# Summing the states of a selective scan by f32 transposes in PSUM, and turning silu(z) instead of the gated result

## The chip, the cores and the metric

The program runs on one core of one Trainium2 chip. The metric is device time in microseconds (us); the kernel before took 230.39 us, the median of three runs (228.88 to 230.66).

## The reference

Two blocks stand one behind the other, for 4 sequences (batches) of 256 positions and 256 channels:

```python
x = x + mixer(ctx_1024, layernorm(x))     # z is layernorm(x)
x = x + ffn(layernorm(x))
# mixer, per batch: 256 channels, 16 states
u  = silu(causal_conv(in_proj(ctx)))
dt = softplus(dt_proj(x_proj(u)) + b)
state = state * exp(dt * A) + (dt * u) * B_t   # a scan over positions, 16 states
y  = sum over states of state * C_t
y  = (y + D * u) * silu(z)
# ffn: h = gelu(silu(quantised linear 256 -> 1024)); layer_norm; quantised linear 1024 -> 256
```

The change concerns the sum over states, the gate by silu(z), and the order of everything around them.

## The kernel before

Channels lie on partitions, in 2 halves (h) of 128; positions lie along the free dimension. The scan is cut into 32 units k: 4 batches (b), 2 halves, 4 groups of 4 states. A unit is 128 x 1024 (4 states x 256 positions), and goes through all engines:

- TensorE (PE): `scale_b(k)`, L474, writes dt*u*B into PSUM, two slots, so it waits for scan k-2;
- ScalarE (ACT): `exps(k)`, L613, four instructions, writes exp(dt*A) into a ring of 6 (`dA`), so it waits for scan k-6;
- VectorE (DVE): `scan(k)`, L909, writes `st`, a ring of 4, so it waits for the sum of unit k-4;
- GpSimd (POOL): `prod(k)`, L753, multiplies `st` by C;
- PE: `sum_states(k)`, L490, adds the four states into one PSUM bank by matmuls with an identity as the stationary operand; ahead of the first unit of each half one matmul with diag(D), L487, adds D*u.

When the four units of a half are summed, DVE multiplies the sum by silu(z) (`gate`, L926, once per half of a batch, out to `yg`), PE transposes the result to positions by channels (`turn_y`, L504, two transposes per call), and DVE adds it to x (`add_x1`, L931). After both halves `ln1` takes statistics, `quant1` quantises, and the FFN runs on tiles t of 128 positions, 8 in all, two per batch: PE `turn_q1`, `mm1` (L527 for the bias, L531); ACT `silu` (L646) and `gelu` (L650), each with a function table of its own; DVE `bn2` (L984); POOL `root2a`; ACT `norm` (L656); DVE `gain` (L1002); POOL `shift` (L789); ACT `square` (L665) and DVE `amax2` (L1009); POOL `root2b`; DVE `scales2`; ACT `scale2` (L671); POOL `quant2`; PE `turn_q2`, ACT `copy_q2` (L678), PE `mm2`, DVE `res`, and a store. ACT computes silu(z) per batch in `silu_z` (L689). Every change of function on ACT to or from exp, silu or gelu loads a table (L707 is the load ahead of `exps`).

The order is written out by hand: for each engine a table (`VECTOR_AT`, `SCALAR_AT`, `POOL_AT`, `PE_AT`) with a row for each unit. An engine does its own part of unit k-1, then what row k names:

```python
for k in range(UNITS + 1):
    if k:
        scan(k - 1)
    for name, i in steps(VECTOR_AT, k):
        work[name](i)
```

Engines run their rows in that order and wait on semaphores only. The last row (32) holds all that stands behind the last scan. One PSUM bank, `head`, is shared by the small PE products and is handed on by `take`; the pair of banks `big` serves `mm1`, `turn_q2` and the convolution.

Of the kernel before, what the change touches and what calls it, by code (L numbers as in the profile page):

```python
# [15 lines left out]
BF16 = mybir.dt.bfloat16  # L16
# [41 lines left out]
    "dt_neg:2 x1:0",
    "spread_b:4 spread_b:5",
    "spread_b:6",  # L60
    "spread_b:7 gate:1 dt_mask:2 dt_sum:2",
# [3 lines left out]
    "x1:1 ln1:0 wmean:0",  # L65
    "spread_b:8 spread_b:9 spread_b:10",
    "gate:2",
    "spread_b:11 clip_weights:0 clip_weights:1 quant1:0 dt_neg:3",
    "gate:3",
    "x1:2 dt_mask:3",  # L70
    "x1:3 ln1:1 bn2:0 dt_sum:3",
# [2 lines left out]
    "quant1:1",
    "gain:0 bn2:1 gate:4",
    "x1:4 spread_b:12 spread_b:13 amax2:0 spread_b:14 bn2:2 gain:1",
    "scales2:0 amax2:1",
    "spread_b:15 gate:5",
    "x1:5 bn2:3 scales2:1 ln1:2",
    "quant1:2 gain:2",  # L80
    "amax2:2 gain:3",
    "bn2:4 scales2:2 amax2:3 gate:6",
    "scales2:3",
    "bn2:5 gain:4 x1:6 gate:7 x1:7 ln1:3 res:0 quant1:3 res:1 amax2:4 scales2:4 gain:5 amax2:5 res:2 "
    "bn2:6 scales2:5 gain:6 res:3 amax2:6 bn2:7 scales2:6 gain:7 quant2:6 res:4 amax2:7 scales2:7 res:5 "
    "quant2:7 res:6 res:7",
)
SCALAR_AT = (
    "silu_u:1",
    "",  # L90
    "copy_xd:1 sum_weights:0",
    "dt_bias:1",
    "copy_half:1",
    "dt_exp:1 silu_u:2",
    "silu_z:0 copy_xd:2 silu_z:1",
    "copy_du:1 dt_bias:2 silu_z:2 dt_exp:2",
# [11 lines left out]
    "silu_u:3",
    "scale_weights:1 copy_xd:3 silu_z:3",
    "dt_bias:3 copy_q1:0 dt_exp:3",  # L110
    "silu:0 gelu:0",
    "norm:0 silu:1 gelu:1 copy_du:3",
    "copy_q1:1",
    "",
    "silu:2 square:0 norm:1 gelu:2 silu:3",
    "",
    "scale2:0 square:1 gelu:3",
    "scale2:1 copy_q2:0 norm:2",
    "norm:3 copy_q2:1",
    "copy_q1:2 square:2 silu:4 gelu:4 square:3 scale2:2",  # L120
    "silu:5 scale2:3 gelu:5 norm:4 square:4 copy_q2:2 norm:5 copy_q2:3 copy_q1:3 scale2:4 silu:6 gelu:6 "
    "square:5 silu:7 scale2:5 gelu:7 square:6 copy_q2:4 scale2:6 copy_q2:5 square:7 copy_q2:6 scale2:7 "
    "copy_q2:7",
)
POOL_AT = (
    "",
    "",
    "",
    "dt_series:1",
    "",  # L130
    "",
    "dt_series:2",
# [981 lines left out]
```

## Time and profile before

| | |
|---|---|
| median of 3 runs | 230.39 us |
| the profiled execution's own time | 231.39 us |
| its span | 229.6 us |
| busy: PE, DVE, ACT, POOL | 193.3, 189.1, 175.3, 144.9 us |
| first scan starts, last scan (unit 31) starts | 26.13, 179.9 us |
| last gate starts | 189.45 us |

The span can be read in three parts: up to 22.7 us inputs arrive and batch 0 is prepared; from there to 179.9 us the 31 scans ahead of the last one and the work between them; and 49.7 us from the last scan's start to the end, where what is left of the FFN runs. Busy time is what an engine spent in its instructions; it is a share of the span and says nothing by itself about which engine ended a wait.

### The profile page before, as it was taken

To read this page: it belongs to the slowest core of one execution; us is meant where nothing else is said; L and a number is where in the kernel's file an instruction comes from. 1 tells how busy PE (TensorE), PEld (TensorE's weight loads), DVE (VectorE), ACT (ScalarE), POOL (GpSimd) and SP (SyncE) were. 2 spreads that over 40 slices of the span, in tenths; PEclk is the share of its full clock that TensorE was granted. 3 is DMA by queue.
4 is the path that set the end of the run, shared out by engine and by line. 5 is a ranking of instruction groups with operands and counts; after the bars stand their busy time and mean duration, and the time that the engine had idled before them with its cause. 6 is when DMAs were issued, how large, how long until landed. Compare 5 with 4: busy or idle time off the path is not lost.

```text
span 229.6 us, 2849 instructions
## 1 busy us (share of the span) xinstructions
PE 193.3 (84%) x886; PEld 146.0 (64%) x886; DVE 189.1 (82%) x266; ACT 175.3 (76%) x269; POOL 144.9 (63%) x142
## 2 busy tenths in 40 slices
PE   3298989989999999999999999939999965892472
PEld 2076668768777898786867877828865753341351
DVE  0985897989999999986999979799999658746861
ACT  2164969988970898897959989996988955779751
POOL 0040037834772976601969099999599998968871
PEclk9999999999999999999999999997999999599569
DMA  6639930004040005410000204300000000100011
GB/s 186 227 85 383 421 144 6 0 0 166 26 178 0 0 0 174 139 58 0 3 0 3 93 6 150 121 0 0 0 0 0 3 0 0 47 23 1 24 46 49
DMA packets 7135, 15.85 MB, mean 69 GB/s; under 512 B 904, under 2 KB 4432, under 8 KB 6992
## 3 DMA queue, kind: packets, MB, share of 16 engines
q1 hardware_dynamic: 6528, 14.90, 18.4%
q10 hardware_dynamic: 592, 0.77, 1.2%
q8 instruction: 7, 0.11, 0.2%
q14 instruction: 8, 0.07, 0.1%
HBM read 14.56 MB, written 1.11 MB: 68 GB/s over the span
## 4 chain that ended last, share of the span: by engine, by line
PE 27%; DVE 21%; POOL 19%; ACT 19%; issue 10%; DMA 1%; POOLq 0%; DVEq 0%; ACTq 0%
POOL st L753 9%; DVE st L909 8%; PE ps L490 6%; ACT dA L613 6%; PE ps L474 6%; PE ps L405 4%; ACT L707 3%; PE ps L527 2%; POOL sm L780 2%; POOL w_raw L789 2%; ACT L689 2%; ACT siluz L689 2%; DVE diagB L894 2%; PE ps L424 1%; DVE sp_mask L856 1%
## 5 line engine op out<-in xcount | busy, mean ns | idle before, releaser
L753 POOL TENSOR_TENSOR st<-st,bc 128x1024 f32<-128x1024 f32 x32 | 75.7, 2374 | 42.7 <-DVE st L909 42.4
L909 DVE TENSOR_TENSOR_SCAN st<-dA,ps 128x1024 f32<-128x1024 f32 x32 | 72.4, 2275 | 3.0 <-PE ps L474 1.6
L474 PE MATMUL ps<-diagB,dtuT 128*128 128x256 f32 x256 | 62.5, 390 | 1.5 <-DVE dtuT L902 0.6
L490 PE MATMUL ps<-st,id_f 128*128 128x256 f32 x256 | 59.7, 381 | 2.3 <-POOL st L753 2.3
L474 PEld LDWEIGHTS ps<-diagB,dtuT 128*128 128x128 f32 x256 | 48.0, 194 | 11.7 <-issue 3.3
L490 PEld LDWEIGHTS ps<-st,id_f 128*128 128x128 f32 x256 | 48.0, 190 | 10.1 <-POOL st L753 3.9
L613 ACT ACTIVATE dA<-dt,negA 128x255 f32<-128x255 f32 x128 | 53.0, 495 | 0.1
L894 DVE TENSOR_TENSOR diagB<-id_f,ps 128x1024 f32<-128x1024 f32 x16 | 18.8, 1202 | 1.5 <-PE ps L424 1.5
L789 POOL TENSOR_TENSOR w_raw<-w_raw,rows_sb 128x1024 f32<-128x1024 f32 x6 | 14.1, 2354 | 7.2 <-DVE w_raw L1002 7.2
L527 PE MATMUL ps<-rows_sb,diag 128*128 128x512 f32 x32 | 17.2, 662 | 0.4 <-ACT w_raw L646 0.4
L984 DVE BATCH_NORM_STATS2 stats<-w_raw 128x6 f32<-128x512 f32 x16 | 10.3, 683 | 6.0 <-ACT w_raw L650 6.0
L538 PE MATMUL ps<-id_b,q 128*128 128x128 bf16 x64 | 6.2, 253 | 10.5 <-ACT q2T L678 6.7
L1009 DVE TENSOR_REDUCE am<-w_raw 128x1 f32<-128x1024 f32 x8 | 9.7, 1216 | 5.9 <-POOL w_raw L789 4.7
L665 ACT ACTIVATE junk<-w_raw 128x1024 bf16<-128x1024 f32 x8 | 8.4, 1050 | 7.6 <-POOL w_raw L789 6.7
L405 PE MATMUL ps<-ctx_sb,taps_sb 128*128 128x256 f32 (+3 forms) x48 | 13.5, 443 | 0.0
L707 ACT ACT_TABLE_LOAD x10 | 12.8, 1283 | 0.2
L538 PEld LDWEIGHTS ps<-id_b,q 128*128 128x128 bf16 x64 | 4.8, 113 | 12.3 <-ACT q2T L678 7.2
L545 PE MATMUL ps<-w2q,q2T 128*128 128x256 bf16 x64 | 10.3, 314 | 2.5 <-DVE res L1034 1.9
L405 PEld LDWEIGHTS ps<-ctx_sb,taps_sb 128*128 128x128 f32 x48 | 10.8, 229 | 2.5 <-issue 0.7
L671 ACT ACTIVATE w_raw<-w_raw,sm 128x1024 f32<-128x1024 f32 x8 | 9.1, 1144 | 3.5 <-DVE sm L1020 3.5
L646 ACT ACT_TABLE_LOAD x8 | 10.3, 1283 | 0.1
L650 ACT ACT_TABLE_LOAD x8 | 10.3, 1283 | 0.1
(120 smaller groups left out, 295.2 us busy)
## 6 DMA issues: line engine op xcount, KB each, us to landing
bc<-spread SPq DMA_DIRECT2D x16, 512.0 KB, 3.6
rows_sb<-rows SPq DMA_DIRECT2D x1, 1664.0 KB, 14.3
x_nat<-x SPq DMA_DIRECT2D x2, 512.0 KB, 7.3
w_raw<-w1T SPq DMA_DIRECT2D x1, 1024.0 KB, 9.0
w_raw<-w2T SPq DMA_DIRECT2D x1, 1024.0 KB, 11.0
out<-res SPq DMA_DIRECT2D x8, 128.0 KB, 1.7
taps_sb<-taps ACTq DMA_DIRECT2D x1, 512.0 KB, 4.9
ctx_sb<-ctxT SPq DMA_DIRECT2D x1, 384.0 KB, 5.5
```

The costliest lines, as they stand in the source:

```text
L405: mm = nc.tensor.matmul(xin(b)[:, h * L + s:(h + 1) * L], inw_taps[:, s, h * P:(h + 1) * P], ctx_sb[:, b * L:(b + 1) * L - s], start=s == ...
L474: mm = nc.tensor.matmul(o[:, i:i + 2, t, :], dtuT[:, b % 2, h, t, :], diagB[:, b % 2, t, n:n + 2, :], start=True, stop=True)
L490: mm = nc.tensor.matmul(yacc, id_f[:, :], st[:, k % ST_RING, i * L:(i + 1) * L], start=False, stop=ng == GROUPS - 1 and i == SG - 1)
L527: nc.tensor.matmul(big[:, c], diag[:, i, :], rows_sb[:, c], start=True, stop=False)
L538: mm = nc.tensor.transpose(tq2[:, k * P:(k + 1) * P], q2[:, t % 2, k * P:(k + 1) * P], id_b[:, :])
L545: mm = nc.tensor.matmul(mm2, q2T[:, t % 2, k, :], w2q[:, k, :], start=k == 0, stop=k == KB - 1)
L613: e = nc.scalar.activation(dA[:, k % DA_RING, i * L + 1:(i + 1) * L], dt[:, h, b % 2, 1:L], ACT.Exp, scale=negA[:, h, n:n + 1])
L707: nc.scalar.preload_act_table_set("natural_log_exp_and_others")
L753: tt(s, s, bc[:, ng].rearrange("p s l -> p (s l)"), ALU.mult).then_inc(prod_done, 1)
L789: tt(h, h, rows_sb[:, 2 * HID:3 * HID], ALU.add).then_inc(shifted, 1)
L894: tt(diagB[:, b % 2, :, n, :], id_f[:, :].unsqueeze(1).unsqueeze(1).to_broadcast([P, TPB, SG, P]), b_cols_of(b)[:, :, n].unsqueeze(3).to_b ...
L909: nc.vector.tensor_tensor_scan(st[:, k % ST_RING, :], dA[:, k % DA_RING, :], slot(k), 0.0, ALU.mult, ALU.add).then_inc(scanned, 1)
```

## The change

The sum over states is made with positions on partitions. Each 128 x 128 block of `st` becomes the stationary operand of an f32 transpose with the identity moving, and eight such transposes per unit accumulate into one bank `yT`, [positions, 2 tiles, 256 channels], which serves both halves. D*u goes there by two matmuls per half. The bank is freed once per batch instead of once per half.

silu(z) is turned instead: PE `turn_z` makes four transposes per batch, ACT `copy_z` copies them to `siluzT`; `gate` and `add_x1` are now per position tile, and `add_x1` reads only SBUF. `turn_y` is gone. `siluz` holds one batch, so `silu_z(b)` waits for `turn_z(b-1)` and is called four times at different places. The scratch output of `square` lies in `taps_sb`, and the last two tiles' shift and quantisation count on semaphores of their own. All four order tables are written anew; of them one line each stands here.

```diff
 VECTOR_AT = (
-    "spread_b:1 spread_b:2",
-    "spread_b:3 dt_half:1",
+    "spread_b:1 dt_half:1",
+    "spread_b:2",
...
 SCALAR_AT = (
-    "silu_u:1",
+    "silu_z:0 silu_u:1",
...
-        yacc = bank(0)[:, 0:L]
+        yT = bank(0).rearrange("p (t d) -> p t d", t=TPB)
...
-                    else:
-                        pe.wait_ge(gate_step, k // GROUPS)
+                    elif h == 0:
+                        pe.wait_ge(gate_step, TPB * b)
                     pe.wait_ge(u_ready, b + 1)
-                    nc.tensor.matmul(yacc, diag_D[:, h, :], u[:, h, b, :], start=True, stop=False)
+                    for t in range(TPB):
+                        nc.tensor.matmul(yT[:, t, h * P:(h + 1) * P], u[:, h, b, t * P:(t + 1) * P], diag_D[:, h, :],
+                                         start=h == 0 and t == 0, stop=False)
                 pe.wait_ge(prod_done, k + 1)
                 for i in range(SG):
-                    mm = nc.tensor.matmul(yacc, id_f[:, :], st[:, k % ST_RING, i * L:(i + 1) * L], start=False,
-                                          stop=ng == GROUPS - 1 and i == SG - 1)
+                    for t in range(TPB):
+                        o = i * L + t * P
+                        mm = nc.tensor.matmul(yT[:, t, h * P:(h + 1) * P], st[:, k % ST_RING, o:o + P], id_f[:, :],
+                                              is_transpose=True, start=False,
+                                              stop=h == 1 and ng == GROUPS - 1 and i == SG - 1 and t == TPB - 1)
                 mm.then_inc(summed, 1)
...
-            def turn_y(g):
-                take("head", x1_half, g + 1)
-                pe.wait_ge(gate_step, g + 1)
-                for i in range(TPB):
-                    mm = nc.tensor.transpose(yT[:, i * P:(i + 1) * P], yg[:, g % 2, i * P:(i + 1) * P], id_f[:, :])
-                mm.then_inc(y_turned, 1)
+            def turn_z(b):
+                take("head", zT_done, b + 1)
+                pe.wait_ge(z_ready, HALVES * (b + 1))
+                for t in range(TPB):
+                    for h in range(HALVES):
+                        mm = nc.tensor.transpose(head[:, t * D + h * P:t * D + (h + 1) * P],
+                                                 siluz[:, h, t * P:(t + 1) * P], id_f[:, :])
+                mm.then_inc(z_turned, 1)
...
+            def copy_z(b):
+                act.wait_ge(z_turned, b + 1)
+                nc.scalar.activation(siluzT[:, b].rearrange("p t d -> p (t d)"), head, ACT.Copy).then_inc(zT_done, 1)
+
             def silu_z(b):
                 act.wait_ge(z_small, 4)
+                if b:
+                    act.wait_ge(z_turned, b)
...
-                tt(yg[:, g % 2, :], yacc, siluz[:, h, b, :], ALU.mult).then_inc(gate_step, 1)
+            def gate(i):
+                b, t = i // TPB, i % TPB
+                dve.wait_ge(summed, UPB * (b + 1))
+                dve.wait_ge(zT_done, b + 1)
+                if i >= TPB:
+                    dve.wait_ge(x1_half, i - TPB + 1)
+                tt(yg[:, t, :], yT[:, t, :], siluzT[:, b, t, :], ALU.mult).then_inc(gate_step, 1)
+
+            def add_x1(i):
+                b, t = i // TPB, i % TPB
+                dve.wait_ge(gate_step, i + 1)
+                tt(x_nat[:, t, b, :], x_nat[:, t, b, :], yg[:, t, :], ALU.add).then_inc(x1_half, 1)
```

What the new tables do to the order is seen on ACT around the last `exps`. Before (L613 is `exps`, L707 its table load, L665 `square`, L646 `silu`, L650 `gelu`, L671 `scale2`, L656 `norm`), the last `exps` is the second L613 row:

```order
L678 ACTIVATE q2T<-ps 128x1024
L613 ACTIVATE dA<-dt,negA 128x255 x4
L636 ACTIVATE q1T<-ps 128x512
L665 ACTIVATE junk,sm<-w_raw 128x1024
L646 ACT_TABLE_LOAD
L646 ACTIVATE w_raw<-ps,sm 128x1024
L650 ACT_TABLE_LOAD
L650 ACTIVATE w_raw<-w_raw 128x1024
L665 ACTIVATE junk,sm<-w_raw 128x1024
L671 ACTIVATE w_raw<-w_raw,sm 128x1024
L707 ACT_TABLE_LOAD
L613 ACTIVATE dA<-dt,negA 128x255 x4
```

Now, in the changed kernel, the same place (L630 is `exps`, L732 its load, L663 `silu`, L667 `gelu`, L690 `scale2`, L673 `norm`, L684 `square`):

```order
L653 ACTIVATE q1T<-ps 128x512
L663 ACT_TABLE_LOAD
L663 ACTIVATE w_raw<-ps,sm 128x1024
L667 ACT_TABLE_LOAD
L667 ACTIVATE w_raw<-w_raw 128x1024
L690 ACTIVATE w_raw<-w_raw,sm 128x1024
L673 ACTIVATE w_raw<-w_raw,sm 128x1024
L732 ACT_TABLE_LOAD
L630 ACTIVATE dA<-dt,negA 128x255 x4
L684 ACTIVATE taps_sb,sm<-w_raw 128x1024
L663 ACT_TABLE_LOAD
L663 ACTIVATE w_raw<-ps,sm 128x1024
```

Three tiles' silu and gelu (2, 3 and 4) now stand in one block ahead of the last `exps` with none of the other `exps` between them, and `square` of tile 2 has moved behind it. Over the whole program ACT has 27 table loads where it had 35.

On PE, before, the last units (L474 `scale_b`, L527 and L531 `mm1`, L504 `turn_y`, L487 the D matmul, L490 `sum_states`):

```order
L527 MATMUL ps<-rows_sb,diag 128x512 x2
L531 MATMUL ps<-w1q,q1T 128x512 x4
L474 MATMUL ps<-diagB,dtuT 128x2x128 x4
L490 MATMUL ps<-st,id_f 128x256 x4
L527 MATMUL ps<-rows_sb,diag 128x512 x2
L531 MATMUL ps<-w1q,q1T 128x512 x4
L474 MATMUL ps<-diagB,dtuT 128x2x128 x4
L504 MATMUL ps<-id_f,yg 128x128 x2
L474 MATMUL ps<-diagB,dtuT 128x2x128 x4
L487 MATMUL ps<-cv,diag_D 128x256
L490 MATMUL ps<-st,id_f 128x256 x16
```

Now, on PE in the changed kernel (L484 `scale_b`, L532 `turn_q1`, L544 and L548 `mm1`, L504 now the accumulating transposes, L498 the D matmuls):

```order
L484 MATMUL ps<-diagB,dtuT 128x2x128 x4
L532 MATMUL ps<-id_b,q 128x128 x4
L544 MATMUL ps<-rows_sb,diag 128x512 x2
L548 MATMUL ps<-w1q,q1T 128x512 x4
L484 MATMUL ps<-diagB,dtuT 128x2x128 x4
L504 MATMUL ps<-id_f,st 128x128 x8
L484 MATMUL ps<-diagB,dtuT 128x2x128 x8
L504 MATMUL ps<-id_f,st 128x128 x8
L544 MATMUL ps<-rows_sb,diag 128x512 x2
L548 MATMUL ps<-w1q,q1T 128x512 x4
L498 MATMUL ps<-diag_D,cv 128x128 x2
L504 MATMUL ps<-id_f,st 128x128 x32
```

`scale_b` of units 29, 30 and 31 stands directly behind tile 4's `turn_q1` and `mm1`, and the first FFN output transposes (`turn_q2`), of which two stood among the last units, all come behind the last sum.

At the start, on DVE, before (L894 `spread_b`, L856 to L876 one half of batch 0's softplus, `dt_half:1`, L909 `scan`):

```order
L902 COPY dtuT<-ps 128x256
L894 TENSOR_TENSOR diagB<-id_f,ps 128x2x512 x2
L909 SCALAR_TENSOR_TENSOR st<-dA,ps 128x1024
L894 TENSOR_TENSOR diagB<-id_f,ps 128x2x512
L856 TENSOR_SCALAR sp_mask<-sp_e 128x256
L858 TENSOR_SCALAR sp_ser<-sp_e 128x256
L860 TENSOR_TENSOR sp_ser<-sp_ser,sp_e 128x256
```

Now, in the changed kernel (L919 `spread_b`, L881 to L901 the half's softplus, L934 `scan`):

```order
L927 COPY dtuT<-ps 128x256
L919 TENSOR_TENSOR diagB<-id_f,ps 128x2x512
L881 TENSOR_SCALAR sp_mask<-sp_e 128x256
L883 TENSOR_SCALAR sp_ser<-sp_e 128x256
L885 TENSOR_TENSOR sp_ser<-sp_ser,sp_e 128x256
L892 COPY_PREDICATED sp_ln<-sp_mask,sp_ser 128x256
L898 SCALAR_TENSOR_TENSOR dt<-sp_v,sp_ln 128x256
L901 TENSOR_TENSOR dtu<-dt,cv 128x256
L934 SCALAR_TENSOR_TENSOR st<-dA,ps 128x1024
```

The second half's softplus has moved ahead of the first scan, and two `spread_b` behind it.

## Rows read from the trace of the kernel before

**Rows 1.** The page's part 1: busy time of each engine over the span.
```profile
PE 193.3 (84%) x886; PEld 146.0 (64%) x886; DVE 189.1 (82%) x266; ACT 175.3 (76%) x269; POOL 144.9 (63%) x142
```

**Rows 2.** The page's part 4: the chain that ended last, by engine.
```profile
PE 27%; DVE 21%; POOL 19%; ACT 19%; issue 10%; DMA 1%; POOLq 0%; DVEq 0%; ACTq 0%
```

**Rows 3.** Windows: length, busy PE, PEld, DVE, ACT, POOL, PEclk, DMA share, GB/s.
```profile
22.70:60.40 37.70, 34.89 (x161) 27.56 (x162) 33.53 (x27) 34.25 (x64) 19.14 (x11) 1.00 0.30 118
60.40:105.70 45.30, 44.52 (x209) 37.20 (x208) 42.18 (x50) 34.65 (x67) 25.03 (x14) 1.00 0.21 71
105.70:140.00 34.30, 33.83 (x154) 24.23 (x153) 32.85 (x45) 29.75 (x42) 24.23 (x22) 1.00 0.10 32
140.00:179.90 39.90, 35.70 (x166) 28.46 (x165) 37.01 (x53) 35.99 (x52) 35.71 (x36) 0.96 0.07 27
179.90:229.60 49.70, 30.14 (x166) 18.88 (x164) 30.83 (x58) 32.70 (x34) 37.48 (x50) 0.83 0.06 22
...
148.40:154.00 5.60, 1.91 (x10) 1.38 (x9) 5.05 (x5) 5.55 (x7) 5.34 (x4) 1.00 0.00 0
154.00:160.00 6.00, 6.00 (x27) 5.22 (x28) 5.90 (x14) 3.98 (x7) 5.42 (x9) 0.72 0.00 0
```

**Rows 4.** Timeline, PE: sums, transposes, mm1 at either clock (start, length, what).
```profile
75.08 0.60 PE L455 MATMUL ps<-id_f,dtu 128*128 128x128 f32 x4
79.45 1.89 PE L490 MATMUL ps<-st,id_f 128*128 128x256 f32 x8
116.72 1.88 PE L527 MATMUL ps<-rows_sb,diag 128*128 128x512 f32 x4
118.43 1.03 PE L531 MATMUL ps<-w1q,q1T 128*128 128x512 bf16 x4
197.12 3.73 PE L527 MATMUL ps<-rows_sb,diag 128*128 128x512 f32 x4
```

**Rows 5.** Timeline, DVE: two waits between 22.7 and 105.7 us.
```profile
39.80 2.29 DVE L909 TENSOR_TENSOR_SCAN st<-dA,ps 128x1024 f32<-128x1024 f32 x1 [1.59 <-PE ps L474]
105.06 0.69 DVE L851 SCALAR_TENSOR_TENSOR sp_e<-sp_v 128x512 f32<-128x512 f32 x1 [2.12 <-ACT sp_v L593]
```

**Rows 6.** Groups of instructions by line, ACT: busy and mean ns, idle before.
```profile
L707 ACT ACT_TABLE_LOAD x10 | 12.8, 1283 | 0.2
L625 ACT ACTIVATE dtuT<-ps 128x512 f32<-128x512 f32 x3 | 1.7, 581 | 8.0 <-PE ps L455 8.0
L646 ACT ACTIVATE w_raw<-ps,sm 128x1024 f32<-128x1024 f32 x8 | 8.9, 1114 | 1.7 <-PE ps L531 1.7
L650 ACT ACTIVATE w_raw<-w_raw 128x1024 f32<-128x1024 f32 x8 | 8.5, 1057 | 0.1
L656 ACT ACTIVATE w_raw<-w_raw,sm 128x1024 f32<-128x1024 f32 x6 | 7.4, 1232 | 3.3 <-POOL sm L782 3.3
L665 ACT ACTIVATE junk<-w_raw 128x1024 bf16<-128x1024 f32 x8 | 8.4, 1050 | 7.6 <-POOL w_raw L789 6.7 <-DVE w_raw L998 0.9
L671 ACT ACTIVATE w_raw<-w_raw,sm 128x1024 f32<-128x1024 f32 x8 | 9.1, 1144 | 3.5 <-DVE sm L1020 3.5
L678 ACT ACTIVATE q2T<-ps 128x1024 bf16<-128x1024 bf16 x8 | 8.1, 1010 | 2.8 <-PE ps L538 2.1 <-PE ps L545 0.7
```

**Rows 7.** Groups of instructions by line, DVE.
```profile
L909 DVE TENSOR_TENSOR_SCAN st<-dA,ps 128x1024 f32<-128x1024 f32 x32 | 72.4, 2275 | 3.0 <-PE ps L474 1.6 <-ACT dA L613 1.4
L931 DVE TENSOR_TENSOR x_nat<-x_nat,ps 128x256 f32<-128x256 f32 x8 | 3.2, 401 | 0.6 <-PE ps L504 0.6
L984 DVE BATCH_NORM_STATS2 stats<-w_raw 128x6 f32<-128x512 f32 x16 | 10.3, 683 | 6.0 <-ACT w_raw L650 6.0
L1002 DVE TENSOR_TENSOR w_raw<-w_raw,rows_sb 128x1024 f32<-128x1024 f32 x6 | 8.8, 1465 | 0.0
L1009 DVE TENSOR_REDUCE am<-w_raw 128x1 f32<-128x1024 f32 x8 | 9.7, 1216 | 5.9 <-POOL w_raw L789 4.7 <-POOL sm L812 1.2
```

**Rows 8.** Waits of ACT in the window 179.9 to 229.6 us.
```profile
ACT junk L665 <- POOL w_raw L789: 5.1, 1, 5.1
```

More of the change, by code:

```diff
@@ L51 @@
 VECTOR_AT = (
-    "spread_b:1 spread_b:2",
-    "spread_b:3 dt_half:1",
-    "dt_neg:1",
-    "",
-    "dt_mask:1 dt_sum:1",
-    "gate:0",
[L58 to L61, printed above, removed]
[35 rows of a table added]
+)
+SCALAR_AT = (
[6 rows of a table added]
     "",
@@ L64 @@
     "",
[L65 to L71, printed above, removed]
-    "",
-    "",
[L74 to L86, printed above, removed]
-)
-SCALAR_AT = (
-    "silu_u:1",
-    "",
[L91 to L96, printed above, removed]
[26 rows of a table added]
+)
+POOL_AT = (
+    "",
+    "",
+    "dt_series:1",
     "",
@@ L101 @@
     "",
-    "copy_du:2 sum_weights:1",
     "",
@@ L105 @@
     "",
-    "scale_weights:0",
     "",
[L108 to L132, printed above, removed]
+    "dt_series:2 root1:0 add_b2:0",
+    "dt_series:3",
     "",
@@ L137 @@
     "",
-    "add_b2:0 root1:0",
+    "root2a:0 add_b2:1 root1:1",
+    "",
+    "root2a:1 shift:0",
+    "",
+    "root2b:0",
+    "",
+    "",
+    "shift:1",
+    "root2b:1 root1:2 quant2:0 out_scale:0 root2a:2",
+    "",
+    "root2a:3 shift:2 quant2:1",
+    "",
+    "",
+    "root2b:2 shift:3 root2a:4 out_scale:1 root1:3 root2a:5 root2b:3 quant2:2 out_scale:2 shift:4 "
+    "quant2:3 add_b2:2 out_scale:3 root2a:6 root2b:4 shift:5 root2a:7 out_scale:4 root2b:5 root2b:6 "
+    "quant2:4 out_scale:5 quant2:5 root2b:7 out_scale:6 add_b2:3 out_scale:7",
+)
+PE_AT = (
+    "xdbl:1 dtraw:1 scale_b:1 turn_half:1 scale_b:2",
+    "turn_z:0 scale_b:3 scale_b:4 convolve:2 wsum:0 scale_b:5",
+    "",
+    "scale_b:6 turn_du:1",
+    "b_cols:1 scale_b:7",
+    "",
+    "scale_b:8",
+    "scale_b:9 turn_z:1",
+    "xdbl:2 scale_b:10 dtraw:2 scale_b:11 b_cols:2 convolve:3 scale_b:12 scale_b:13 xdbl:3",
+    "turn_du:2",
+    "dtraw:3",
+    "",
+    "turn_z:2 scale_b:14 scale_b:15 turn_q1:0",
+    "mm1:0 b_cols:3 scale_b:16 scale_b:17",
+    "",
+    "scale_b:18",
+    "scale_b:19 scale_b:20 mm1:1",
+    "",
+    "",
+    "scale_b:21",
+    "turn_du:3 scale_b:22",
+    "scale_b:23 turn_z:3 scale_b:24 scale_b:25 turn_q1:1",
+    "",
+    "",
+    "scale_b:26 mm1:2 scale_b:27",
+    "mm1:3",
+    "scale_b:28 turn_q1:2 mm1:4 scale_b:29",
+    "scale_b:30 scale_b:31",
+    "mm1:5",
     "",
@@ L548, in _ @@
             work = {"convolve": convolve, "wsum": wsum, "xdbl": xdbl, "dtraw": dtraw, "b_cols": b_cols, "turn_du": turn_du,
-                    "turn_half": turn_half, "turn_y": turn_y, "turn_q1": turn_q1, "mm1": do_mm1, "scale_b": scale_b,
+                    "turn_half": turn_half, "turn_z": turn_z, "turn_q1": turn_q1, "mm1": do_mm1, "scale_b": scale_b,
                     "turn_q2": turn_q2, "mm2": do_mm2}
```

103 lines of the change are left out of this document (24 added, 79 removed), and 60 rows, old and new, of tables (SCALAR_AT, VECTOR_AT).

## The prediction, made before the changed kernel was run

> **What bounds the kernel now.** I read the busy shares first [rows 1]: PE 84%, DVE 82%, ACT 76%, POOL 63%. No engine stands out, and the chain that ended last changes engine all the time [rows 2]. So the question goes to the stages, and the table by stretch answers it [rows 3]. I cut at the first row of the order tables (22.7 us) and at the start of the last scan (179.9 us). Between them lie 157.2 us, in which PE was busy 34.89+44.52+33.83+35.70 = 148.9, DVE 33.53+42.18+32.85+37.01 = 145.6, ACT 134.6 and POOL 104.1. PE and DVE are thus both nearly full: PE hardly waits between 60 and 140 us (78.4 of 79.6 busy), and DVE's idle time is only 157.2 - 145.6 = 11.6 us. The last stretch, 49.7 us, is another case: the busiest engine there (POOL) works 37.5 us, ACT 32.7, DVE 30.8. It is a chain of small steps between engines, and the sum over states has no part in it after its first 10 us.
>
> The reader should take one thing from this: the span is 22.7 + (DVE's work ahead of the last scan) + (DVE's idle time there) + (the rest after the last scan starts) = 22.7 + 145.6 + 11.6 + 49.7 = 229.6. Whatever PE or ACT save can shorten the span only through the 11.6 and the 49.7. The execution took 231.39 us on its own clock, 1.8 over its span, and 1.0 over the median of the runs.
>
> **The change part by part: PE.** A unit's sum took 1.89 us for 8 records of 256 columns [rows 4]. The new sum is 8 f32 transposes of 128 columns. The nearest row is L455, f32 transposes from SBUF: 4 in 0.60 us [rows 4]. One record lasts about 0.27 from start to end, so each further one adds (0.60-0.27)/3 = 0.11, and eight take 0.27 + 7 x 0.11 = 1.04 us. No row shows a transpose that accumulates. Bounds: 1.04 if accumulation is free, 1.89 (saving nothing) if it costs a second pass; below, nothing speaks for less. I take 1.04, since the row has the same operands and kind. Saved: 0.85 a unit; about 29 sums lie ahead of the last scan, 24.7 us. The D matmuls (one of 256 columns becomes two of 128) and `turn_z` against `turn_y` (4 x 4 transposes for 8 x 2) I take as even, within 1 us either way. PE's work ahead of the last scan falls from 148.9 to about 124. It stops being a bound, DVE does not.
>
> **ACT.** Eight table loads fewer (35 to 27), 8 x 1.283 = 10.3 us [rows 6]; four `copy_z` more at L625's 0.58, 2.3 us; the scattered `silu_z` and their loads are in that count. Net -8.0 us of 175.3.
>
> **DVE.** `gate` and `add_x1` stay 8 instructions each of 128 x 256, about 0.40 us [rows 7]. `add_x1` now has both operands in SBUF; I take no price. Bounds: nothing, or up to 0.5 us each where POOL works beside it, 4 us in all (L1002, two SBUF operands, ranges that way: its mean of 1.47 for 1024 elements is above L1009's 1.22). What counts is what the new order moves behind the last scan: `bn2:4` (2 x 0.68), `gain:3` (1.47), `amax2:3` (1.22), `gate:6` (0.40) and two pairs of tiny scale steps, together 4.8 us [rows 7]. DVE's work ahead of the last scan: 145.6 - 4.8 = 140.8.
>
> **DVE's idle time ahead of the last scan.** 22.7 to 60.4: 4.2 us, of which 1.59 is scan 3 waiting for its `scale_b`, which stood behind the 16 records of a convolution [rows 3, 5]. Now `scale_b:3` stands ahead of the convolution, and `dt_half:1` fills the gap ahead of scan 0: 1.5 left. 60.4 to 105.7: 3.1, of which 2.12 is `dt_neg:3` waiting for a bias step on ACT [rows 5]; it now stands after scan 12 with shorter queues on PE: 1.0 left. 105.7 to 140: 1.5, kept. 140 to 179.9: 2.9, and here a new wait arises. The block of silu and gelu for tiles 2 to 4 stands ahead of the last `exps`. From the end of `quant1:2` ACT needs a copy 0.58, `mm1:4` on PE 2.74 (116.72 to the end at 119.46 [rows 4]), silu 1.11, a load and gelu 2.34, scale2 1.14, norm 1.23, a load 1.28 and four exps 1.98: 12.4 us. DVE meanwhile has a scan 2.28, stats 1.37, amax 1.22, gain 1.47, two scans 4.55, amax 1.22: 12.1 [rows 6, 7]. `norm:2` (1.23) stands ahead of the copy, so the last scan waits about 1.5 us; queued behind it on DVE is the whole of row 32, for which everything waits. With the old 2.9 partly gone, 3.0. Sum: 7. Bounds: 4 (every old wait gone, the new one half hidden) and 11.6 (as now). I take 7.
>
> **After the last scan starts.** ACT gets `square:2` and `:3`, `scale2:2`, `copy_q2:0` and `:1` from ahead of the scan: 2 x 1.05 + 1.14 + 2 x 1.01 = 5.3 us [rows 6]; POOL gets a shift, a quantisation and their roots. ACT waited 5.1 us there for POOL [rows 8], a hole which the moved work can fill in part; but POOL, the busiest engine, grows as well. Bounds: 49.7 (all in holes) and 58 (all on top, and the low clock in more of it). I take 53.5.
>
> **Sum.** 22.7 + 140.8 + 7 + 53.5 = 224.0 us of span, 225.8 on its own clock, and 1.0 less as a median: 225.
>
> **The clock.** From 148.4 to 154 PE was busy 1.91 of 5.6 us, and in the next 6 us the granted clock averaged 0.72: part of it at 1.2 GHz instead of 2.4 [rows 3]. At 197 us the four L527 records take 3.73 us instead of 1.88 [rows 4]. In the changed kernel PE has still less to do ahead of the last scan, and waits at tile 4's `turn_q1` in just that place. The Trainium skill ("TensorE: Matmul & The Clock Gate", Part 4: PE-mode transpose) says that transposes do not count as PE activity and leave the clock low. No row here has transposes alone for long enough to show it. What a low clock would do to this kernel is the fourth case below, worked out from the rows alone.
>
> **The rivals.**
>
> 1. Forecast, 225: above. Its own range is 218 (4 us idle, 49.7 after: 217.2 of span) to 229.
>
> 2. No change, about 230: PE's relief is hidden because DVE's idle time has causes of its own (11.6 stays), or the transposes take 1.89 a unit when they accumulate, so that the change does not do what it says. 22.7 + 140.8 + 11.6 + 54 = 229.1, median 229.9. For it: in 60 to 140 us DVE idles under 5 us, whatever PE does. Against it: its waits there were on things that the order moves.
>
> 3. Slower, about 235: the last `exps` behind the block on ACT (three silu, three gelu and their loads alone are 3 x 2.39 + 3 x 2.34 = 14.2 us [rows 6]). If `gelu:2`, `norm:2` and `mm1:4` each come late (a 1.2 GHz clock adds 1.85 to L527 alone, and `scale_b:29` to `:31` are queued behind it on PE), the last scan waits some 6.5 us instead of 1.5. With the other waits as now: 22.7 + 140.8 + 16.6 + 54.5 = 234.6, median 235.4. It decides from an idle time of 12.6 us on, when the last scan starts later than 176.1. Against it: DVE has 12.1 us of work of its own meanwhile, and ACT may run ahead of it by six units.
>
> 4. Slower, about 243: the clock. PE's 124 us of work with a third at half speed (the sums, 33 us, and the `scale_b` next to some of them) is 165; PE becomes the bound again and 22.7 + 165 + 53.5 = 241, median 242. For it: the low clock behind the hole at 148.4. Against it: PE keeps 124/157 = 79% of its time busy, and sums and transposes lie between f32 matmuls nearly everywhere.
>
> **How the numbers follow.** Forecast 0.64, no change 0.18, last exps 0.11, clock 0.07. A measurement of this kernel tells 1% (2.3 us) from no change, about. Faster by more than that: 0.64; within: 0.18; slower: 0.18. The range reaches from 218 (the low bounds of both terms) to 233 (22.7 + 140.8 + 11.6 + 58 = 233.1), into case 3 but not through it.
>
> **What would show it right or wrong.** In the profile of the changed kernel: the accumulating transposes at 1.0 to 1.1 us for eight, and PE some 27 us less busy in all; ACT near 167 us; DVE near 189, as now; the last scan starting at 168 to 173 us; DVE idle near 7 us between 22.7 and there; then 52 to 55 us to the end. The forecast is wrong if the transposes take more than 1.5 us for eight, if the last scan starts after 176, with ACT's `exps` named as what it waited for, if the granted clock is under 0.9 ahead of the last scan, or if the rest takes over 57 us.

## The result, and the profile after

| | before | changed |
|---|---|---|
| median, same chip | 230.15 us | 219.53 us |
| ratio, 95% interval | | 0.9528 [0.9439, 0.9616] |
| changed kernel timed again, on another chip | 230.56 us | 220.53 us, ratio 0.9586 [0.9541, 0.9631] |

The kernel became 4.1 to 4.7% faster: 10 to 10.6 us, where 5.4 were forecast. The profiled execution took 222.06 us, one of the longer of the kernel's; where a number hangs on that, the profile of the second set (219.37 us, span 217.6) stands beside it. Executions of one kernel differ here by 1 to 4%, mostly along with the granted clock, so a profile stands for one execution, and its own time is given beside the median below.

The page's parts 1 and 4 of the changed kernel:

```profile
PE 170.9 (78%) x902; PEld 129.0 (59%) x902; DVE 188.6 (86%) x266; ACT 167.0 (76%) x265; POOL 146.8 (67%) x142
DVE 38%; PE 25%; POOL 20%; issue 14%; DMA 1%; ACT 1%; POOLq 0%; DVEq 0%
```

Against [rows 1] PE lost 22.4 us and ACT 8.3; DVE and POOL kept theirs within 2 us. Against [rows 2] the chain that ended last goes through DVE for 38% (21% before), and ACT has left it (19% to 1%).

Windows of the changed kernel: first row of the order tables to the last scan, the rest, and the first part in stretches (columns as in [rows 3]):

```profile
22.20:163.90 141.70, 125.09 (x674) 98.26 (x675) 139.24 (x161) 119.72 (x210) 101.49 (x72) 0.98 0.19 70
163.90:220.30 56.40, 31.84 (x192) 21.25 (x190) 36.65 (x69) 38.12 (x41) 41.99 (x59) 0.76 0.06 19
22.20:60.00 37.80, 35.62 (x204) 29.72 (x204) 37.32 (x34) 36.28 (x74) 21.11 (x10) 1.00 0.39 147
60.00:105.00 45.00, 41.69 (x221) 33.33 (x222) 43.52 (x50) 33.74 (x64) 31.63 (x19) 0.96 0.14 48
105.00:140.00 35.00, 28.81 (x161) 22.04 (x159) 34.79 (x42) 28.72 (x52) 28.43 (x23) 1.00 0.16 61
140.00:163.90 23.90, 18.97 (x90) 13.17 (x91) 23.61 (x38) 20.97 (x23) 20.32 (x22) 0.93 0.00 1
```

The last scan starts at 163.9 us in place of 179.9. Of the 141.7 us ahead of it DVE worked 139.24 and idled 2.5 (1.6 in the second profile; 11.6 in [rows 3], counted there from 22.7 us). PE idles 16.6 there, and ACT 22. The last stretch grew from 49.7 to 56.4 us.

The changed kernel's groups by line: the new sum, the scan, POOL's product, `scale_b` (busy, mean ns, idle before):

```profile
L504 PE MATMUL ps<-id_f,st 128*128 128x128 f32 x256 | 31.9, 273 | 1.1 <-POOL st L778 1.1
L934 DVE TENSOR_TENSOR_SCAN st<-dA,ps 128x1024 f32<-128x1024 f32 x32 | 72.0, 2273 | 1.4 <-PE ps L484 1.3
L778 POOL TENSOR_TENSOR st<-st,bc 128x1024 f32<-128x1024 f32 x32 | 77.4, 2437 | 32.0 <-DVE st L934 31.9
L484 PE MATMUL ps<-diagB,dtuT 128*128 128x256 f32 x256 | 63.5, 393 | 9.6 <-DVE st L934 8.6
```

and two of them before, POOL's product and `scale_b`:

```profile
L753 POOL TENSOR_TENSOR st<-st,bc 128x1024 f32<-128x1024 f32 x32 | 75.7, 2374 | 42.7 <-DVE st L909 42.4
L474 PE MATMUL ps<-diagB,dtuT 128*128 128x256 f32 x256 | 62.5, 390 | 1.5 <-DVE dtuT L902 0.6 <-DVE st L909 0.6 <-issue 0.3
```

The scan's waits fell from 3.0 [rows 7] to 1.4 us. PE's `scale_b` now waits 8.6 us for the scan, where it waited 0.6 before. POOL's product waited for the scan in both kernels, 42.4 and 31.9 us.

Timeline of the changed kernel: one unit's sum on PE; the last `exps` on ACT and the last scan on DVE:

```profile
31.49 1.04 PE L504 MATMUL ps<-id_f,st 128*128 128x128 f32 x8
```
```profile
162.12 1.70 ACT L630 ACTIVATE dA<-dt,negA 128x255 f32<-128x255 f32 x4
163.91 2.29 DVE L934 TENSOR_TENSOR_SCAN st<-dA,ps 128x1024 f32<-128x1024 f32 x1
```

Eight transposes that accumulate take 1.04 us, as eight that don't accumulate were worked out to. The last `exps` end at 163.82, 0.1 us ahead of the last scan, which follows DVE's own step without a wait.

### The profile page after: what moved, and what is told of

Read it like the earlier page. It is cut to its first block, busy times and chain, and to the rows that moved or that the text cites. A ratio compares the mean times of both kernels' runs of the same rounds, so it can differ in the third digit from the quotient of the medians.

```text
span 220.3 us, 2873 instructions
## 1 busy us (share of the span) xinstructions
PE 170.9 (78%) x902; PEld 129.0 (59%) x902; DVE 188.6 (86%) x266; ACT 167.0 (76%) x265; POOL 146.8 (67%) x142
## 4 chain that ended last, share of the span: by engine, by line
DVE 38%; PE 25%; POOL 20%; issue 14%; DMA 1%; ACT 1%; POOLq 0%; DVEq 0%
DVE st L934 17%; PE ps L484 8%; PE ps L415 4%; DVE diagB L919 4%; POOL st L778 4%; POOL w_raw L814 3%; PE ps L504 3%; PE ps L562 2%; POOL sm L835 2%; POOL q L843 2%; DVE stats L1008 2%; PE ps L555 2%; POOL sm L807 1%; PE ps L445 1%; POOL sm L805 1%
## 5 line engine op out<-in xcount | busy, mean ns | idle before, releaser
L778 POOL TENSOR_TENSOR st<-st,bc 128x1024 f32<-128x1024 f32 x32 | 77.4, 2437 | 32.0 <-DVE st L934 31.9
L934 DVE TENSOR_TENSOR_SCAN st<-dA,ps 128x1024 f32<-128x1024 f32 x32 | 72.0, 2273 | 1.4 <-PE ps L484 1.3
L484 PE MATMUL ps<-diagB,dtuT 128*128 128x256 f32 x256 | 63.5, 393 | 9.6 <-DVE st L934 8.6
L484 PEld LDWEIGHTS ps<-diagB,dtuT 128*128 128x128 f32 x256 | 47.3, 193 | 20.0 <-DVE st L934 12.2
L630 ACT ACTIVATE dA<-dt,negA 128x255 f32<-128x255 f32 x128 | 52.6, 495 | 1.2 <-DVE dt L898 1.1
L504 PE MATMUL ps<-id_f,st 128*128 128x128 f32 x256 | 31.9, 273 | 1.1 <-POOL st L778 1.1
L504 PEld LDWEIGHTS ps<-id_f,st 128*128 128x128 f32 x256 | 28.7, 141 | 3.1 <-POOL st L778 1.9
L562 PE MATMUL ps<-w2q,q2T 128*128 128x256 bf16 x64 | 11.9, 348 | 8.9 <-ACT q2T L697 5.4
L919 DVE TENSOR_TENSOR diagB<-id_f,ps 128x1024 f32<-128x1024 f32 x16 | 18.8, 1204 | 0.0
L544 PE MATMUL ps<-rows_sb,diag 128*128 128x512 f32 x32 | 17.6, 679 | 1.1 <-DVE w2q L943 0.8
L555 PE MATMUL ps<-id_b,q 128*128 128x128 bf16 x64 | 7.9, 299 | 9.7 <-POOL q L843 5.6
L562 PEld LDWEIGHTS ps<-w2q,q2T 128*128 128x128 bf16 x64 | 7.4, 123 | 12.3 <-issue 6.3
L555 PEld LDWEIGHTS ps<-id_b,q 128*128 128x128 bf16 x64 | 6.6, 139 | 11.2 <-issue 5.9
L690 ACT ACTIVATE w_raw<-w_raw,sm 128x1024 f32<-128x1024 f32 x8 | 9.2, 1146 | 4.6 <-DVE sm L1044 4.4
L684 ACT ACTIVATE taps_sb<-w_raw 128x1024 bf16<-128x1024 f32 x8 | 8.4, 1048 | 5.0 <-POOL sm L822 2.6
L415 PEld LDWEIGHTS ps<-ctx_sb,taps_sb 128*128 128x128 f32 x48 | 10.6, 226 | 2.4 <-issue 0.7
L697 ACT ACTIVATE q2T<-ps 128x1024 bf16<-128x1024 bf16 x8 | 8.1, 1017 | 4.2 <-PE ps L555 4.1
L663 ACT ACTIVATE w_raw<-ps,sm 128x1024 f32<-128x1024 f32 x8 | 8.9, 1114 | 2.3 <-PE ps L548 2.2
L667 ACT ACT_TABLE_LOAD x8 | 10.3, 1283 | 0.1
```

The costliest lines, as they stand in the source:

```text
L415: mm = nc.tensor.matmul(xin(b)[:, h * L + s:(h + 1) * L], inw_taps[:, s, h * P:(h + 1) * P], ctx_sb[:, b * L:(b + 1) * L - s], start=s == ...
L484: mm = nc.tensor.matmul(o[:, i:i + 2, t, :], dtuT[:, b % 2, h, t, :], diagB[:, b % 2, t, n:n + 2, :], start=True, stop=True)
L504: mm = nc.tensor.matmul(yT[:, t, h * P:(h + 1) * P], st[:, k % ST_RING, o:o + P], id_f[:, :], is_transpose=True, start=False, stop=h == 1 ...
L544: nc.tensor.matmul(big[:, c], diag[:, i, :], rows_sb[:, c], start=True, stop=False)
L555: mm = nc.tensor.transpose(tq2[:, k * P:(k + 1) * P], q2[:, t % 2, k * P:(k + 1) * P], id_b[:, :])
L562: mm = nc.tensor.matmul(mm2, q2T[:, t % 2, k, :], w2q[:, k, :], start=k == 0, stop=k == KB - 1)
```

## The experiments

Every span below is cut into the same three parts, nearly as in the prediction: what DVE works from 22.2 us (there 22.7) to the start of the last scan, what it idles there, and the rest. The parts are from the windows of one profiled execution, whose own time stands beside them; the medians are over all executions.

| kernel | DVE busy ahead | idle ahead | rest | the profiled one, us | median us |
|---|---|---|---|---|---|
| before | 145.9 | 11.8 | 49.7 | 231.4 | 230.4 |
| changed (first, second profile) | 139.2, 137.4 | 2.5, 1.6 | 56.4, 56.4 | 222.1, 219.4 | 219.5, 220.5 |
| `half_sum` | 144.3 | 14.7 | 47.6 | 230.6 | 229.1 |
| `quarter_sum` | 145.4 | 11.8 | 47.5 | 228.9 | 232.9 |
| `old_order` | 147.5 | 17.5 | 50.7 | 239.8 | 243.1 |
| `plain` | 137.5 | 9.3 | 55.3 | 226.2 | 226.7 |
| `loads` | 136.4 | 8.7 | 55.5 | 224.6 | 224.6 |
| `plain_loads` | 138.7 | 13.1 | 55.7 | 231.5 | 230.8 |
| `dve_plus` | 146.2 | 3.9 | 55.3 | 229.4 | 229.5 |
| `dve_plus_before` | 149.9 | 10.2 | 49.4 | 233.5 | 233.4 |
| `warm` | 139.6 | 2.4 | 59.5 | 225.5 | 223.6 |
| `shift_dve` | 137.8 | 3.8 | 51.9 | 217.5 | 215.4 |
| `shift_warm` | 137.5 | 3.8 | 56.1 | 221.4 | 221.3 |

**Relief of PE in the old order (`half_sum`), the new order without it (`plain`), the new sum in the old order (`old_order`), the changed kernel again (`same`).**

```diff
half_sum, in the kernel before
-                for i in range(SG):
+                for i in (0, SG - 1):
plain, in the changed kernel
-                                              is_transpose=True, start=False,
+                                              start=False,
old_order, in the changed kernel: all order tables of before, with turn_z and copy_z
in the places of turn_y's steps, and silu(z) kept in siluzT until it is turned
-                                                 siluz[:, h, t * P:(t + 1) * P], id_f[:, :])
+                                                 siluzT[:, b, h, t * P:(t + 1) * P], id_f[:, :])
```

> The kernel before, with its own order, but sum_states adds only two of the four states of each unit: 4 records of 256 columns fewer per unit, about 0.95 us, slightly more than the transposes save (0.85). It leaves two states out of every sum. Theory A (PE's relief reaches the end only where the order lets it; under the old order DVE's waits have other causes): 225 to 230 us, at most 2% under the kernel before. Theory B (PE's relief alone is the gain): 219 to 222 us, as the changed kernel.

> The changed kernel, with the same order, but the eight 128 x 128 blocks are summed by ordinary f32 matmuls instead of transposes: two records each, 16 per unit, about 1.95 us as in the kernel before. Theory A (the order alone brings most of it, DVE is the bound and PE has room): 219 to 223 us. Theory B (without PE's relief the new order cannot run, PE is again the bound): 226 to 232 us.

> The changed sum, gate and turned silu(z), but with the order tables of the kernel before (gates and adds of a batch moved to where its second one stood, turn_z in the places of turn_y, copy_z behind copy_du and copy_q1). ACT has 35 table loads again and four copies more, PE 25 us less. Theory A: 225 to 230 us. Theory B: 219 to 222 us.

> The changed kernel once more, for a second profile and more times: 218 to 222 us. If the spread of its times comes from the TensorE clock in the part after the last scan, a profile with a shorter time shows the same start of the last scan (163 to 164 us) and fewer slow mm1 and mm2 records behind it.

Measured: `half_sum` 229.08 us, ratio 0.9895 [0.9845, 0.9946]; `plain` 226.68, 0.9856 [0.9818, 0.9895]; `old_order` 243.1, 1.0457 [1.0403, 1.051]; `same` 220.53, 0.9586. `half_sum` lies in the range of its theory A. `plain` lies in that of its theory B: the order alone does not bring most of the gain. `old_order` is slower than either of its theories allowed. For `same` I expected the last scan at 163 to 164 us in a shorter execution too, and the difference behind it; it was the other way round: the last scan starts at 161.2 and the rest is 56.4 us again. The windows up to the last scan, of `half_sum`, of `plain`, and of `same`:

```profile
22.20:181.10 158.90, 132.65 (x569) 99.17 (x573) 144.25 (x171) 134.27 (x223) 104.15 (x81) 0.95 0.17 61
```
```profile
22.20:169.00 146.80, 143.16 (x892) 122.51 (x896) 137.53 (x160) 119.64 (x209) 100.83 (x72) 1.00 0.18 67
```
```profile
22.20:161.20 139.00, 123.53 (x672) 98.15 (x676) 137.44 (x162) 119.99 (x211) 102.33 (x72) 0.99 0.20 70
```

In `plain` PE is busy 143.2 of 146.8 us: in the new order, with ordinary matmuls, PE is again nearly full. In `half_sum` PE idles 26 us, and DVE waits no less than before. But that profile is of an execution of 230.62 us at a granted clock of 0.924. Two others, not profiled, took 225.83 us at 0.953 and 226.22 at 0.938, 4.3 to 4.7 us under the kernel before: where the clock stayed up, half the relief did show in the old order. `old_order` puts z's steps where I chose, so it is no fair test of the tables, and neither does it show what the new sum would be worth in the old order with better places; it shows that this arrangement costs 5%. Which of its places costs what was not pursued.

**More relief in the old order (`quarter_sum`).** Three of four states are left out of the sum.

```diff
-                for i in range(SG):
+                for i in (SG - 1,):
```

> The kernel before, with its order and its 35 table loads, in which one of each row's four states is summed; three are left out. Its sum then costs TensorE about what the transposes cost in the changed one (125 us ahead of the last scan in place of 149). With 35 loads the same relief brought the new order from 230.8 to 224.6, 6 us. Theory A (what counts is how much TensorE is relieved; the half relief was too small): 224 to 226. Theory B (the old order's rows, each with turns and products placed by other due times, hold VectorE up at ScalarE's steps whatever TensorE does): 227 to 230, with VectorE's waits of 10 us or more ahead of the last scan left as they are.

Measured: 232.94 us in the median, ratio 1.0131 [1.0092, 1.017]: with a quarter of the sum's matmuls it is no faster than before, and the median is outside both ranges. The five executions took 228.87, 232.51, 232.94, 233.57 and 235.06 us. The profile is of the first of these. Part 1 of its page, and the waits of DVE up to its last scan (us in total, times, longest):

```profile
PE 164.4 (72%) x694; PEld 115.1 (51%) x694; DVE 188.8 (83%) x266; ACT 175.3 (77%) x269; POOL 145.1 (64%) x142
```
```profile
DVE st L909 <- PE ps L474: 4.8, 2, 3.3
DVE dtuT L902 <- PE ps L447: 2.7, 1, 2.7
DVE am L1009 <- POOL w_raw L789: 1.9, 2, 1.6
DVE sp_e L851 <- ACT sp_v L593: 1.2, 2, 0.9
```

The scans wait 4.8 us for `scale_b` (1.6 in the kernel before, 3.0 in `half_sum`), though PE has 22 us less to do ahead of them. The longest of these waits is at 41.33 us. The window ahead of it (granted clock 0.50), the convolution that stands ahead of the `scale_b` on PE, and the scan:

```profile
34.70:38.10 3.40, 3.40 (x9) 2.70 (x8) 3.35 (x3) 3.37 (x10) 2.66 (x1) 0.50 0.03 10
34.28 5.29 PE L405 MATMUL ps<-ctx_sb,taps_sb 128*128 128x256 f32 x16
41.33 2.29 DVE L909 TENSOR_TENSOR_SCAN st<-dA,ps 128x1024 f32<-128x1024 f32 x1 [3.28 <-PE ps L474]
```

In the kernel before the same 16 records took 3.60 us at full clock and the scan behind them waited 1.59 [rows 5]. The second wait, 1.48 us at 123.8, likewise stands behind a stretch at 0.50 (120.0 to 123.4 us). So part of what PE no longer had to do came back as a slower PE, at matmuls that a scan waits for. This is the kind of loss that the prediction's fourth case was about, in another kernel and smaller. The granted clock of the four longer executions was 0.873 to 0.881, that of the profiled one 0.900 (before about 0.955). Theory A is out. Theory B fits the profiled execution in both its signs, 228.87 us and 11.8 us of idle time; the other executions lie above its range and have no profile. How much of the cost is the order and how much the clock stays open; the two executions of `half_sum` above say that the clock is a good part of it.

**The two savings apart and together (`loads`, `plain_loads`).**

```diff
loads, in the changed kernel; plain_loads has the edit of plain too
+                    if k in (4, 8, 13, 17, 19, 22, 26, 29):
+                        nc.scalar.preload_act_table_set("natural_log_exp_and_others")
```

> The changed kernel with ScalarE's table loads put back: eight more loads (35 again, as before the change) ahead of the exps at eight places before the last scan, so ScalarE has 8 x 1.283 = 10.3 us more to do there. Nothing else moves, and nothing is left out of the computation. Theory A (ScalarE had room, and its saving carried little of the gain): 219.5 to 222, within 2 us of the changed kernel's 219.5 to 220.5. Rival B (the gain rests on ScalarE's shorter rows, since exps and rms steps then come in time for the scans): 225 to 230, with VectorE waiting for dA or w_raw in its list of waits.

> The changed kernel with both savings put back: the sums over states by ordinary f32 matmuls in place of transposes, and eight table loads of ScalarE, 35 in all; its order of the work stays. Nothing is left out. Apart they cost 226.7 - 220.5 = 6 us and 224.6 - 220.5 = 4 us. Theory A (each of the two engines is late at scans of its own, so the costs add): 229 to 232, the time of the kernel before, and the new order by itself brings nothing. Rival (both fill the same waits of VectorE): 226.5 to 228, and the new order by itself brings some 3 us.

Measured: `loads` 224.63 us, ratio 0.9694 [0.9649, 0.9739]; `plain_loads` 230.77, 0.9996 [0.9955, 1.0037]. Theory A of `loads` falls (2 us at most), its rival fits but for 0.4 us: of ACT's 10.3 us about 4 come back (4.1 by the medians; 2.5 by the ratios, each to the kernel before on its own chip). In its profile DVE waits 1.5 us for dA and 2.4 for w_raw. Theory A of `plain_loads` holds: with both savings undone the new order takes the time of before. The window and the waits of DVE up to the last scan of `plain_loads`:

```profile
22.20:174.00 151.80, 145.69 (x896) 124.27 (x899) 138.70 (x162) 131.87 (x219) 100.66 (x72) 0.99 0.18 65
```
```profile
DVE st L936 <- PE ps L484: 4.1, 5, 1.6
DVE dtuT L929 <- PE ps L457: 3.1, 1, 3.1
DVE st L936 <- PE ps L504: 2.8, 2, 2.1
DVE st L936 <- ACT dA L630: 1.5, 1, 1.5
```

The order takes 7.2 us of DVE's work from ahead of the last scan (145.9 to 138.7) and gives 6.0 back behind it (49.7 to 55.7): no gain, as long as PE and ACT are as full as before. What is left between the four kernels is idle time: 13.1 with neither saving, 9.3 with ACT's alone, 8.7 with PE's alone, 2.5 or 1.6 with both. Each engine is late at steps of its own, so the costs add.

**Is DVE now the bound? (`dve_plus`, `dve_plus_before`).** The same edit in either kernel: six of the spreadings are done twice (long arguments are shortened to "...").

```diff
+                if b and g % 2:
+                    tt(diagB[:, b % 2, :, n, :], id_f[:, :]...
+                       b_cols_of(b)[:, :, n]..., ALU.mult).then_inc(again, 1)
+                    dve.wait_ge(again, 2 * (b - 1) + g // 2 + 1)
```

> The changed kernel with VectorE's work made longer: the odd channel groups of the spreading of B over the diagonals of batches 1 to 3 are done twice, 6 more of some 1.2 us = 7.2 us more of VectorE ahead of the last scan; the second writes the same values, nothing is left out. Theory A (VectorE alone now bounds the stretch up to the last scan, so its busy time passes to the end one to one): 226.5 to 228. Rival (TensorE or ScalarE still paces the rows as well, and part of it is hidden): 220 to 224.

> The same doubled work, 7.2 us more of VectorE ahead of the last scan, in the kernel before the change. Theory A (there VectorE waits 11.6 us in that stretch for others, mostly TensorE and ScalarE, and the added work fills part of the waits): 232 to 235, that is 2 to 5 us more than the kernel before. Rival (the waits are a fixed chain behind VectorE's own work, and the work passes to the end in full): 237 to 238.

Measured: `dve_plus` 229.5 us, ratio 0.9921 [0.9898, 0.9945], 9.0 over `same` (7.7 by the ratios); `dve_plus_before` 233.43, 1.0104 [1.0071, 1.0137], 2.7 over before. The 7.2 us cost at least all of themselves in the changed kernel, and a third in the one before: theory A both times, its range for the first passed by 1.5 us. The windows up to the last scan, of `dve_plus` and of `dve_plus_before`:

```profile
22.20:172.30 150.10, 130.06 (x674) 100.91 (x679) 146.17 (x167) 119.59 (x210) 103.15 (x73) 0.95 0.18 65
```
```profile
22.20:182.30 160.10, 148.73 (x681) 117.38 (x685) 149.92 (x176) 134.41 (x222) 104.29 (x81) 0.99 0.17 61
```

In the kernel before only 1.6 us of the added 7.2 went into idle time. DVE's busy time grew by 4.0, not 7.2: other steps of DVE became shorter by 3 us. In `dve_plus` it grew by 8.8 over `same`, more than was added. That led to the last section.

**The last stretch (`warm`, `shift_dve`, `shift_warm`).** It grew to 56.4 us, with a granted clock of 0.76 and POOL its busiest engine. `warm` fills PE's waits there; `shift_dve` gives tiles 4 and 5 the two fused operations of DVE that tiles 6 and 7 had; of its edit the line with the constant is shown, and the semaphore counts of those tiles follow it. `shift_warm` is both.

```diff
warm, in the changed kernel
+                if k == UNITS:
+                    pe.wait_ge(scanned, UNITS)
                 for name, i in steps(PE_AT, k):
+                    if k == UNITS:
+                        for _ in range(4):
+                            nc.tensor.matmul(slot(0)[:, 0:512], id_b[:, :], w1q[:, 0, 0:512], start=True, stop=True)
                     work[name](i)
shift_dve, in the changed kernel
-        LAST = TILES - TPB
+        LAST = TILES - 2 * TPB
```

> The changed kernel with four added bf16 matmuls of 512 columns, whose results nobody reads, ahead of each item of TensorE behind the last sum over states; the first of them wait for the last scan. They fill TensorE's waits in the last stretch, where the granted clock is 0.73 to 0.76. Theory A (the low clock costs the last stretch: its matmuls to the second product take 1.9 us instead of 1.04 there): 216 to 219, with a granted clock above 0.85 there. Rival (TensorE's matmuls there lie beside GpSimd's and VectorE's rms steps, so the clock costs nothing, and the added ones, 4 x 0.21 us, now and then stand ahead of real ones): 220 to 224.

> The changed kernel with one change of mine: tiles 4 and 5 get their normalization and shift as tiles 6 and 7 do, by VectorE's two fused operations from PSUM, and no longer by ScalarE (2 x 1.2 us) and GpSimd (2 x 2.35 us); VectorE gets some 2.7 us in place of nothing. Nothing is left out. If GpSimd's queue sets the last stretch (the chain of waits gives it 20%): 215 to 218. If VectorE does: 221 to 223.

> Both changes of mine at once: tiles 4 and 5 shifted by VectorE (215.4 alone) and the added matmuls behind the last scan. Nothing is left out. If the low clock costs the last stretch: 211 to 214. If not: 215 to 219.

Measured: `warm` 223.62 us, ratio 0.9661 [0.9583, 0.9739]; `shift_dve` 215.41, 0.933 [0.928, 0.938]; `shift_warm` 221.31, 0.9594 [0.9544, 0.9644]. The last stretch of `warm` and, from its timeline, a piece of PE in it (L583 are the added matmuls):

```profile
164.20:223.70 59.50, 41.89 (x263) 25.21 (x266) 36.67 (x69) 37.97 (x41) 41.99 (x59) 0.94 0.05 19
```
```profile
209.68 1.06 PE L555 MATMUL ps<-id_b,q 128*128 128x128 bf16 x8
210.53 1.81 PE L583 MATMUL ps<-w1q,id_b 128*128 128x512 bf16 x4
212.18 1.04 PE L562 MATMUL ps<-w2q,q2T 128*128 128x256 bf16 x8
```

The clock rose from 0.76 to 0.94, and the time did not fall: the median is 3 to 4 us longer, though the intervals of `warm` and of the changed kernel overlap. `shift_warm` against `shift_dve` makes it clear: 5.9 us longer (0.9594 against 0.933), outside both ranges that I had given, with a last stretch of 56.1 us at a clock of 0.94 in place of 51.9 at 0.77. The added matmuls stand ahead of real ones on PE and sometimes run at 1.81 us; the second product above waits for them, and DVE's waits for that product grew from 6.0 (6.8 in the second profile) to 9.1 us. So `warm`'s rival is right in this. What a full clock alone would be worth there can't be read from these runs. The last stretch of `shift_dve`:

```profile
163.80:215.70 51.90, 28.17 (x186) 19.46 (x186) 38.86 (x70) 35.68 (x39) 37.75 (x56) 0.77 0.06 21
```

POOL has 4.2 us less there, ACT 2.4 less, DVE 2.2 more; the stretch is 4.5 us shorter at the same low clock. The run takes work off ACT as well; but in the changed kernel the chain that ended last lies on POOL from 164.9 to 206.7 us, but for 1.5 us of DVE, and nowhere there on ACT. So POOL's queue did set it, as the first expectation had it. Of all kernels timed this is the fastest: 6.7% under the kernel before, about 2.3% under the changed one.

## Why the prediction was right in direction and wrong in size

**The cut was useful.** Span = start + DVE's work + DVE's idle time + rest comes out in any kernel, by the way it is cut; what was tested is that DVE's work passes to the end in full in the changed kernel (`dve_plus`). By terms: 22.7 became 22.2; 140.8 became 139.2; 7 became 2.5; 53.5 became 56.4. The span came to 220.3 in place of 224.0, and the median lies 2.5 us under the profiled execution in place of 1.0; that 1.5 us is chance, in the second set the median lies 1.2 us over it. In the second profile the terms are 22.2, 137.4, 1.6 and 56.4. Of the signs, the last scan came earlier (163.9 us) than the 168 to 173 named, and the rest was just over its 52 to 55.

**The step that failed is "DVE's idle time ahead of the last scan", the term of 7 us.** I summed 1.5 + 1.0 + 1.5 + 3.0 = 7. Measured were 2.5 and 1.6, under my lower bound of 4. Two faults. First, the new wait of 1.5 us for the last `exps` hardly arose. In the first profile it was nothing, and that is partly luck: DVE's two `diag` steps just ahead took 2.60 us (see the last section) and ACT waited 1.27 us for `mm1:4`. In the second profile they took 0.48, and the wait was 0.39:

```profile
148.68 0.48 DVE L1002 TENSOR_SCALAR diag<-id_f,sm 128x128 f32<-128x128 f32 x2
161.19 2.29 DVE L934 TENSOR_TENSOR_SCAN st<-dA,ps 128x1024 f32<-128x1024 f32 x1 [0.39 <-ACT dA L630]
```

There ACT ended its `exps` 12.3 us after `quant1:2` with `norm:2` in that time, where I had 12.4 and `norm:2` on top: I had put all of `mm1:4` behind ACT's copy, but its bias matmuls ran beside `norm:2`, and the rest beside the load for silu. Second, and more: I took away only waits that I could name in a list, and kept "1.5, kept" for the rest. ACT's saving of 8 us stood in the prediction without a use of its own in this term, that is at nothing. What the runs show is that both savings act on the idle time: `plain`, `loads` and `plain_loads` price them at about 4 us of time for ACT's relief, 6 for PE's, 10 for both, and from 13.1 us of idle time with neither to 2.5 with both. My reading of this, which no run shows step by step, is that a wait is what is left after an engine's lead over DVE has been used up, so that a lead of both takes away nearly all waits and not only those in the list.

**The sum's price (1.04 us) was right**: 31.9 us for 256 records, and PE's work ahead of the last scan is 125.1 for the 124 forecast. In all PE lost 22.4 us and not "some 27": behind the last scan its busy time rose from 30.1 to 31.8, at a granted clock of 0.76 (before 0.83). ACT's 167.0 for 167 was right too. `add_x1`, which I had put at no price, took 4.1 us in place of 3.2 [rows 7]: two of its eight took 0.93 us, beside POOL, which is the 0.5 each that I had named as the bound.

**DVE's work, 140.8 forecast, 139.2 and 137.4 measured.** I had 4.8 us moved behind the last scan. With the same work on PE and ACT as before, the part ahead of it is 7.2 us shorter (`plain_loads`), but not all of that was moved: some 2 us of it is time for which DVE was held up by POOL (9.8 us in this part before, 7.7 in `plain_loads`, 9.2 and 7.1 in the two profiles of the changed kernel; how this is counted stands in the last section). Without it DVE's work there fell by 5.2 to 6.1 us, near the 4.8 forecast. The rest is by luck, and it is also most of what the two profiles of the changed kernel differ by.

**The rest after the last scan was 2.9 us short.** I filled ACT's hole of 5.1 us with moved work and put the forecast in the middle of the bounds; but POOL's queue is the path there (`shift_dve`), so what the order moved onto POOL counted: its 37.5 us became 42.0. 6.7 of the 8.3 us at most came.

**The rivals.** No change (idle time has its own causes): wrong for the changed kernel, but it is what the profiles of both relief runs in the old order showed, 14.7 and 11.8 us of idle time, at lower clocks. The last `exps` late: no, a wait of nothing and of 0.39 us in the two profiles. The clock: 0.98 ahead of the last scan, where PE idled 16.6 of 141.7 us, so no; in `quarter_sum`, where it idled 29.8 of 157.2, it was 0.90. The Trainium skill's rule ("TensorE: Matmul & The Clock Gate", Part 4: PE-mode transpose), by which transposes leave the clock low, isn't decided here: `plain` ran at 0.945 to 0.955 and the changed kernel at 0.915 to 0.938, but `plain` also kept PE busier.

## What to carry to other kernels

When several engines are nearly full, cut the span by the one that has to do its work in order, and ask of every saving on the other engines what it does to that idle time, beyond the waits that can be named in a list. Test the parts of a change by undoing one and then both: here the new order alone brought nothing, and the two savings in it 4 and 6 us. When such a test leaves out work, look at the granted clock of every execution before reading its time. After such a change look at once at the stretch that grew: here moving two tiles' steps off the busiest engine there gave 2% more.
